# A routed feed-forward behind cross-attention: pauses between row scatters, three late weight transfers moved, one PSUM bank for each tile of results

## What is computed

```python
x = x + cross_attention(layernorm(x), ctx)        # x is (8, 256, 256), ctx is (8, 1601, 256)
xf = layernorm(x).reshape(2048, 256)              # N = 2048 tokens, H = 256
base_y = silu_mul(xf @ base_gate_up) @ base_down  # shared expert, inner size 512
probs = softmax(xf @ gate_w); w, idx = top_k(probs, 2); w = w / w.sum(-1)
for e in range(8):
    out += comb[:, e] * (silu_mul(xf @ expert_gate_up[e]) @ expert_down[e])
x = x + out + base_y
```

## Time and profile before

| | |
|---|---|
| median of 3 runs | 1282.35 us (1281.01 to 1284.29) |
| the profiled execution | 1287.55 us |
| its span | 1285.7 us |
| PE busy | 1218.9 us (95%) |
| DVE busy | 789.2 us (61%) |
| ACT busy | 689.3 us (54%) |
| POOL busy | 371.1 us (29%) |
| transfers | 228.88 MB, mean 178 GB/s |

### The profile page before, as it was taken

The page is one execution under the profiler, slowest core; times in us unless marked ns, Lnnn a source line. Parts: engine busy times, 40 slices in busy tenths (PEclk is TensorE's granted clock), DMA queues, the critical chain, the costliest instruction groups (busy, mean ns, idle before and its releaser), DMA issues. The chain is left out here.

```text
span 1285.7 us, 23224 instructions
## 1 busy us (share of the span) xinstructions
PE 1218.9 (95%) x8550; PEld 917.1 (71%) x8550; DVE 789.2 (61%) x1630; ACT 689.3 (54%) x954; POOL 371.1 (29%) x282
## 2 busy tenths in 40 slices
PE   6899999999999999999999999999998889899994
PEld 5767777777777777777777777756546778688883
DVE  5266676767767777677777777777737334244442
ACT  4436666666666666675666666656663222222231
POOL 4403223322322432233233222211204531133331
PEclk8879999999999999999999999999999989899998
DMA  6766576678768667776866677564517739733323
GB/s 193 230 172 177 168 204 168 185 211 220 218 192 232 181 190 220 206 214 208 238 172 166 191 195 192 191 166 108 130 58 274 288 103 322 230 55 59 59 46 86
DMA packets 164510, 228.88 MB, mean 178 GB/s; under 512 B 65568, under 2 KB 134568, under 8 KB 164336
## 3 DMA queue, kind: packets, MB, share of 16 engines
q1 hardware_dynamic: 149952, 194.80, 52.8%
q0 software_dynamic: 9216, 16.46, 6.0%
q10 hardware_dynamic: 5232, 16.13, 3.6%
HBM read 133.56 MB, written 95.68 MB: 178 GB/s over the span
## 5 line engine op out<-in xcount | busy, mean ns | idle before, releaser
L628 DVE TENSOR_REDUCE mx<-side 128x1 f32<-128x400 f32 (+1 forms) x1024 | 534.7, 569 | 143.5 <-PE side L403 134.9
L495 ACT ACTIVATE prob<-st 128x1024 f32<-128x1024 f32 (+1 forms) x416 | 412.6, 1023 | 182.7 <-PE st L424 181.0
L403 PE MATMUL side<-kst,qst 96*128 96x400 f32 (+1 forms) x1024 | 331.4, 384 | 6.7 <-DVE mx L628 3.2
L403 PEld LDWEIGHTS side<-kst,qst 96*128 96x128 f32 x1024 | 190.8, 190 | 118.0 <-issue 38.1
L424 PE MATMUL st<-qst,kst 97*128 97x512 f32 (+1 forms) x832 | 265.4, 402 | 5.7 <-ACT prob L495 3.5
L436 PE MATMUL acc<-prob,v 128*32 128x256 f32 (+1 forms) x3328 | 206.4, 383 | 0.0
L424 PEld LDWEIGHTS st<-qst,kst 97*128 97x128 f32 (+1 forms) x832 | 148.4, 186 | 18.2 <-ACT prob L495 9.0
L436 PEld LDWEIGHTS acc<-prob,v 128*32 128x32 f32 (+1 forms) x3328 | 95.2, 110 | 78.4 <-issue 22.2
L660 POOL TENSOR_TENSOR clo<-raw,chi 128x768 fp32r<-128x768 f32 (+1 forms) x32 | 60.8, 1901 | 299.0 <-ACT chi L526 299.0
L666 POOL TENSOR_TENSOR flo<-fc,fhi 128x768 fp32r<-128x768 f32 (+1 forms) x32 | 61.2, 1912 | 204.1 <-ACT fhi L539 204.1
L1543 POOL DMA_INDIRECT token_sums<-yg,xg x39 | 60.9, 1561 | 169.7 <-DMA token_sums<-yg,xg 88.5
(11 more groups left out here) (194 smaller groups left out, 1675.7 us busy)
## 6 DMA issues: line engine op xcount, KB each, us to landing
kst<-parts_at SPq DMA_DIRECT2D x90, 400.2 KB, 5.9
parts_at<-parts SPq DMA_DIRECT2D x48, 384.0 KB, 6.7
wall<-w_at ACTq DMA_DIRECT2D x10, 1536.0 KB
w_at<-piece_hi SPq DMA_DIRECT2D x27, 512.0 KB, 6.6
w_at<-piece SPq DMA_DIRECT2D x27, 512.0 KB, 5.9
v<-v_at SPq DMA_DIRECT2D x32, 408.0 KB
raw<-ctx_t SPq DMA_DIRECT2D x24, 384.0 KB, 5.2
piece<-gate_up SPq DMA_DIRECT2D x18, 512.0 KB, 5.0
```

Of the source, the lines that this page charges most:

```text
L403: pe.matmul(side[u.bank][:, 0:w], t.qst[0:96, pair, col * P:(col + 1) * P], t.kst[0:96, pair, o:o + w], start=True, stop=True).then_inc(si ...
L495: act.activation(prob[0:rows, s, :], st[(KT * g + s) % 2][0:rows, :], ACT.Exp, scale=float(DH) ** -0.5).then_inc(exp_done, 1)
L628: dve.tensor_reduce(mx[:, p % 2, hq, r:r + 1], side[u.bank][:, 0:RANGES[r][1]], AX.X, ALU.max)\
```

## The change

There are three edits. (1) POOL, in the middle of each eight scatters, waits until the first four have landed. (2) Three late parts, both of expert 7 and the first of expert 6, are issued by ACT one behind the other right after its last `shared_high` of the last chunk, ahead of `turn_x(0)` and without a wait for scatters or y stores; the other seven are issued in the routed tiles 0 to 6, behind the same two waits as before. (3) Token tile q of each chunk goes into bank py[q], so PE waits for the reader of tile n - 4, not of tile n - 2. Since py[2] and py[3] hold logits and counts at first, PE waits for routed ahead of tile 2 of the first chunk. `last_down` waits for the reader of the bank that it rewrites.

```diff
--- before.py
+++ after.py
@@ -1270,6 +1270,9 @@
 
 ALL_IN = 16
 
+FIRST_LATE = [(7, 0), (7, 1), (6, 0)]
+THEN_LATE = [(e, a) for e in (3, 4, 5, 6) for a in range(2) if (e, a) not in FIRST_LATE]
+
 
 SLOT_TILES = (TOP * N + E * (P - 1)) // P
 XG = 6
@@ -1446,7 +1449,7 @@
             for q in some:
                 i = TQ * c + q
                 eng.wait_ge(y_full, i + 1)
-                part_y = (py[q % 2] if c < TC - 1 else last_y[q])[:, 0:D]
+                part_y = (py[q] if c < TC - 1 else last_y[q])[:, 0:D]
                 if c < POOL_TC:
                     part_y = y_copy[q]
                     eng.wait_ge(y_copied, i + 1)
@@ -1529,6 +1532,9 @@
                             .then_inc(rows_ready, 1)
                         pool.wait_ge(rows_ready, ready + 2)
                         for i in some:
+                            if i == some.start + T // 4:
+
+                                pool.wait_ge(rows_out[half], 8 * T * k + 16 * T // 4)
                             pool.indirect_dma_start(
                                 out=slot_x, out_offset=bass.IndirectOffsetOnAxis(ap=slots[:, i, k:k + 1], axis=0),
                                 in_=rows[:, i, :], in_offset=None).then_inc(rows_out[half], 16)
@@ -1689,7 +1695,7 @@
                     for q in range(TQ):
                         i = TQ * c + q
                         act.wait_ge(y_full, i + 1)
-                        act.activation(y_copy[q], py[q % 2][:, 0:D], ACT.Copy).then_inc(y_copied, 1)
+                        act.activation(y_copy[q], py[q][:, 0:D], ACT.Copy).then_inc(y_copied, 1)
 
                 act.wait_ge(sub_done, 1)
                 act.activation(ex[:, :, :], ex[:, :, :], ACT.Exp).then_inc(gate_exp, 1)
@@ -1712,6 +1718,10 @@
                         if f > 0:
                             shared_high(c, f - 1)
                     shared_high(c, FT - 1)
+
+
+                for e, a in FIRST_LATE:
+                    load_part(act, place(e), w_at, e, a, late_in)
                 turn_x(0)
 
                 def turn_h(n):
@@ -1733,9 +1743,9 @@
                         for rows_half in rows_out:
                             act.wait_ge(rows_half, 8 * TOP * T)
                         act.wait_ge(y_out, 16 * TC)
-                    if n < 2 * (E - EARLY):
-                        e = EARLY + n // 2
-                        load_part(act, place(e), w_at, e, n % 2, late_in)
+                    if n < len(THEN_LATE):
+                        e, a = THEN_LATE[n]
+                        load_part(act, place(e), w_at, e, a, late_in)
                 turn_h(SLOT_TILES - 1)
 
             @block.tensor
@@ -1773,12 +1783,15 @@
                     pe.wait_ge(hl_done, FT * (c + 1))
                     for q in range(TQ):
                         n = TQ * c + q
-                        after(pe, y_copied if n - 2 < TQ * POOL_TC else y_done, n - 1)
+                        if c == 0 and q == 2:
+
+                            pe.wait_ge(routed, 1)
+                        after(pe, y_copied if n - 4 < TQ * POOL_TC else y_done, n - 3)
                         i = 0
                         for a, part in ((hh, 0), (hh, WE), (hl, 0)):
                             for f in range(FT):
                                 at = part + WD + f * D
-                                mm = pe.matmul(py[q % 2][:, 0:D], a[:, f, q * P:(q + 1) * P], wb[:, at:at + D],
+                                mm = pe.matmul(py[q][:, 0:D], a[:, f, q * P:(q + 1) * P], wb[:, at:at + D],
                                                start=(i == 0), stop=(i == 3 * FT - 1))
                                 i += 1
                         mm.then_inc(y_full, 1)
@@ -1798,8 +1811,8 @@
 
                     pe.wait_ge(hl_done, FT * TC - 1)
                     for q in range(TQ - 1):
-                        if q < 2:
-                            pe.wait_ge(y_done, T - TQ - 1 + q)
+
+                        pe.wait_ge(y_done, T - 2 * TQ + py.index(last_y[q]) + 1)
                         last_results(q, range(FT - 1))
                     pe.wait_ge(hl_done, FT * TC)
                     for q in range(TQ - 1):
```

## The result

The changed kernel takes 1288.2 us (median of 12 runs, 1285.59 to 1291.87) against 1282.11 us of the kernel before (12 runs, 1279.01 to 1285.6): 6.1 us longer, a ratio of 1.0046 with a 95% interval of 1.003 to 1.0062. It is slower, and the forecast was 3 us faster; the time lies above the range of 1272 to 1286.5. In the sessions further down, one execution of the kernel before (1447.16 us) and one of the version without the fourth pause (5190.54 us) were far slower than all others and are left out of the ratios.

A forecast was written before the change was run, and what follows sets the result against it. PE was taken as the limit (busy 95%) except in the shared expert and the early routed tiles, where it idles. 2.3 + 2.5 - 7.8 = -3.0 us: 1284.5 us profiled, 1279.4 for the median; range 1272 to 1286.5.

The forecast's parts named there:

- What the tiles gain: Routed tiles: with 7 parts passing and not 10, 1.3 of 9.1 us lost stay: -7.8 us (bounds -3 and -9.1).
- The pauses and the parts beside the last group: Scatters ahead of routed tiles: pauses 2.9 + 3 x 1.4 = 7.1 us, three parts beside the last group +3.0 us.
- bound by the DMA engines alone, 1.6 us each: First scatter group, beside early weights: each scatter takes 1.6 us, two halves 9.1 us each, so its pause costs +2.9 us.
- The first transposes: Start of turn_x on PE: rows in at 1057.1 against 1054.79, so +2.3 us, and PE waits for them.
- The gain of 7.9 us: PE ahead of the first transposes: 3.6 + 1.8 + 2.5 = 7.9 us earlier, at 1046.9, but hidden under the wait for rows.
- late signals: Last tile of chunk 2: matmuls end at 1038.6, DVE and ACT see it only at 1041.7; the pause might end this.
- Its reason for the clock: Ahead of the last down product: after about 2.1 us idle the clock stays up, 36 matmuls take 4.3 us, not 6.8.
- The half clock: PE behind the long wait for the first rows: clock halved as from 1048.00 to some 1053.3, costing +2.5 us.
- The change in us is carried over: Whole kernel: sum made against the profiled 1287.55 us, its change in us applied to the median, 5.2 us lower.
- B: From ACT's three issues to turn_x(0): first rows become the bound, +11.8 us, in all +6.5 us, 1288.9; chance 0.14.
- A: Last scatters: parts pass beside them without harm, rows in at 1052.6, in all -8.5 us, 1273.9; chance 0.28.
- The packet rule of the Trainium skill: DMA queues: an engine takes turns a whole packet at a time, so small rows wait behind long ones; no size given.

The follow-up runs named there:

- the two looks: Two further single profiled executions of the kernel before, with nothing changed: 1279.56 and 1280.96 us.

## Why the prediction was wrong, point by point

- **What the tiles gain** (-7.8 us). Right: 8.8 us between the two profiled executions, 8.4 and 9.9 us against the two looks. The load ended with the seventh part, and POOL caught up, though later than described: the DMA engines still move 363 GB/s until 1105, and only from 1109.08 on do the accumulates follow each other in 4.6 us or less, under a tile's time.
- **The pauses and the parts beside the last group** (7.1 + 3.0 = 10.1 us). Mis-sized. By the length of the four groups, after against before: 20.9 against 15.5 us, 13.8 against 12.3, 13.3 against 12.6, and 19.1 against 11.9, together 14.8 us. The groups in the middle grew by 1.5 and 0.8 us, about the 1.4 us of the sum. The first cost 5.4 us and not 2.9, the last group grew by 7.2 us and not by 1.4 + 3.0. The failed step is "bound by the DMA engines alone, 1.6 us each": with two, four and eight issued ahead of the wait, the landing beside weights took 5.65, 5.63 and 5.57 us. The upper end of the prediction's own range for the first pause, 5.3 us, the whole landing less 0.30, was the right value.
- **The first transposes** (+2.3 us). This step failed most. The forecast was 1057.1 and 1062.43 was measured, 7.6 us and not 2.3 behind 1054.79. And it set the new time of the rows against 1054.79, a PE time of the profiled execution that stood 8 us behind its rows. In the looks the first transposes start at 1047.14 and 1048.00, and PE arrives between 2 us behind the rows and 0.5 us ahead of them, so hardly any slack was there to absorb a delay. The gain of 7.9 us that the prediction gave PE, by banks and by an end of the late signals, was for the most part no gain of the change: ordinary executions reach the transposes as early, even at half clock. Its reason for the clock, that an idle time of about 2 us leaves it up, came true in this trace and not in nine others.
- **The half clock** (+2.5 us). It came, behind the 14.78 us, and was over sooner: the clock was back about 2.9 us after PE started again, not 5.3. From the first transposes to tile 0 it is 3.04 us against 1.66 and 1.70 in the looks, so it cost 1.4 us.
- **"The change in us is carried over"** to the median. Here the wrong sign arose. Against the execution that was read, the forecast was -3.0 us and the measured -0.1. Against an ordinary one tile 0 starts 14.1 us later (72.2 us after the first scatter against 58.1) or 14.8 (57.4), and the tiles give back 8.4 or 9.9: +5 to +6 us, which is about the 6.1 us measured. So of the 8.8 us between the forecast of 1279.4 and the 1288.2 measured, some 3 are the sizes above, and about 6 are time that the execution that was read lost ahead of tile 0 and that ordinary ones don't lose.
- **The rivals.** B was the right side: slower, decided between ACT's three issues and `turn_x(0)`, with transposes past 1060.1. Its price was put together from a slow accumulate and a slow row load; what came was a latency at each of two pauses under load, with a first row load that took only 2.1 us. That its 1288.9 us lies so near the measured 1288.2 is luck: it stood for a loss of 6.5 us against the execution that was read, and there the loss was nil. A's case for itself, that the second group began beside weights and lost nothing, didn't carry over. The packet rule of the Trainium skill that spoke for B (DMA: Bandwidth & Descriptors, "Queues, rings and completion order") agrees with the long landings in direction; that packets take turns, and why two scatters need as long as eight, no run here shows.
- **The late signals.** They are absent from the two looks of before and from every other profiled execution of the study, with pauses or without, so the pauses can't be what ended them. What makes them stays open.

What each edit does to the kernel before: pauses 9.8 us slower; three parts and banks nothing; parts and banks together 2.4 us slower. The whole is 6.1 us slower and not more than the pauses alone. The two traces show why: with the parts moved, tile 0 starts 5.7 us later still (72.2 against 66.5 us after the first scatter), but the tiles take 203.2 us and not 215.9.

## What to carry to other kernels

Before an edit is priced from one profiled execution, compare its time with the runs: this one was longer than each of the twelve runs timed with it, and what it had too much were just the waits that one of the edits seemed to remove and the slack that the other two seemed to have. A wait for a transfer to land costs that landing as it is at that place and time, here 1.7 us when the engines are free and 5.6 us beside weights, and splitting a group pays it again. Where transfers share the engines, moving some earlier moves the delay to whoever passes there; ask of the new place what is the next thing waited for.

## What wasn't expected of the hardware

Beside weight transfers at 414 GB/s the last of two, four or eight scatters landed some 5.6 us after the end of its issue, whatever their number. A store of 512 KB took 14.7 us to land beside three parts of 1,536 KB issued on another queue 2 us ahead of it.

Behind the same idle time of 2.01 us ahead of the last down products, PE's granted clock fell from 1.00 to 0.50 (from 2.4 to 1.2 GHz) in nine profiled executions and stayed at 1.00 in four (the changed kernel, the pauses alone, the banks alone, the change with the old banks). The 36 matmuls behind it took 5.9 to 6.1 us in the one case and 4.5 in the other. What decides it, no run here shows.
